# A four-stage network kernel: software-pipelined loop replaced by a written-out order over eight batches

## What is computed

```
x = x + attn_a(layernorm(x))   # 16 heads of 8, rotary q and k, causal over 256 rows
x = x + ffn(layernorm(x))
x = x + attn_b(layernorm(x))   # causal inside groups of 32 rows, q and k rms-normalised
x = x + ffn(layernorm(x))      # same weights as the first ffn
# ffn: h = silu(q4(x) @ q4(w_gate).T) * (q4(x) @ q4(w_up).T); out = q4(h) @ q4(w_down).T
# q4: blocks of 16 scaled by max|x|/6 and rounded to the FP4 grid 0 .5 1 1.5 2 3 4 6
```

## Time and profile before

| | us |
|---|---|
| median of 3 runs | 627.68 |
| lowest and highest run | 624.8, 632.15 |
| span of the profiled execution | 621.5 |
| VectorE busy / TensorE busy / ScalarE busy | 354.9 / 387.6 / 203.7 |
| mean granted TensorE clock | 0.834 |

### The profile page before, as it was taken

The page is one execution under the profiler, slowest core; times in us unless marked ns, Lnnn a source line. Parts: engine busy times, 40 slices in busy tenths (PEclk is TensorE's granted clock), DMA queues, the critical chain, the costliest instruction groups (busy, mean ns, idle before and its releaser), DMA issues.

```text
span 621.5 us, 11084 instructions
## 1 busy us (share of the span) xinstructions
PE 387.6 (62%) x4031; PEld 249.4 (40%) x4061; DVE 354.9 (57%) x950; ACT 203.7 (33%) x548; POOL 168.9 (27%) x210
## 2 busy tenths in 40 slices
PE   0316656756966796678677866785788438516533
PEld 0214434534543554455444544454445324303312
DVE  3406667267249844985497449755954637431532
ACT  1000603512640374146404640564155204302300
POOL 6110210430243044214430443143222212320201
PEclk9957969968895999599968996998689759955955
DMA  5050140072018002800370037004600130040000
GB/s 170 0 120 2 32 90 2 23 159 47 1 52 170 6 2 65 165 3 0 88 141 3 0 84 146 3 0 102 122 4 2 45 66 3 9 102 2 10 0 8
DMA packets 61951, 31.84 MB, mean 51 GB/s; under 512 B 3360, under 2 KB 61664, under 8 KB 61920
## 3 DMA queue, kind: packets, MB, share of 16 engines
q1 hardware_dynamic: 61920, 31.42, 22.9%
HBM read 17.19 MB, written 13.63 MB: 50 GB/s over the span
## 4 chain that ended last, share of the span: by engine, by line
PE 44%; DVE 25%; issue 8%; DMA 6%; POOL 6%; ACT 6%; SPq 4%; POOLq 0%; DVEq 0%; ACTq 0%
PE bank L619 6%; PE bank L637 4%; PE bank L517 3%; PE bank L585 3%; PE bank L577 3%; PE bank L502 3%; PE bank L465 3%; DMA Kl<-scr_l 2%; DVE bmax L972 2%; PE bank L432 2%; PE bank L444 2%; PE bank L506 2%; PE bank L630 2%; PE bank L572 2%; PE bank L541 2%
## 5 line engine op out<-in xcount | busy, mean ns | idle before, releaser
L972 DVE TENSOR_REDUCE bmax<-bank 128x3 f32<-128x384 f32 x128 | 63.0, 552 | 24.1 <-PE bank L487 22.8
L693 ACT ACTIVATE prob<-bank 128x384 f32<-128x384 f32 x128 | 55.9, 490 | 12.1 <-PE bank L506 11.0
L483 PE MATMUL bank<-Kf,Qf 128*128 128x128 bf16 x128 | 23.5, 281 | 53.9 <-DMA Kf<-scr_f 45.7
L828 POOL TENSOR_TENSOR fa__w<-fa__w,fa__c 128x256 f32<-128x256 f32 (+1 forms) x16 | 19.2, 1202 | 116.4 <-DVE fa__w L932 116.4
L828 POOL TENSOR_TENSOR fb__w<-fb__w,fb__c 128x256 f32<-128x256 f32 (+1 forms) x16 | 19.9, 1242 | 92.9 <-DVE fb__w L932 92.9
L733 ACT ACTIVATE probl<-bank 128x512 f32<-128x512 f32 x64 | 38.3, 599 | 19.2 <-PE bank L577 18.1
L483 PEld LDWEIGHTS bank<-Kf,Qf 128*128 128x128 bf16 x128 | 10.1, 113 | 72.5 <-DMA Kf<-scr_f 30.9
L485 PE MATMUL bank<-Kf,Qf 128*128 128x256 bf16 x128 | 35.5, 374 | 0.0
L487 PE MATMUL bank<-maskb,identb 128*128 128x256 bf16 x128 | 34.9, 369 | 0.0
L577 PE MATMUL bank<-Ql,Kl 51*128 51x128 bf16 x256 | 26.1, 224 | 11.7 <-DMA Ql<-nmTl 9.5
L656 ACT ACTIVATE fa__xqT<-bank 128x256 f32<-128x256 f32 x8 | 3.1, 385 | 84.1 <-PE bank L432 84.1
(11 more groups left out here) (208 smaller groups left out, 966.4 us busy)
## 6 DMA issues: line engine op xcount, KB each, us to landing
scr_f<-partsf SPq DMA_DIRECT2D x16, 192.0 KB, 2.3
Qf<-scr_f SPq DMA_DIRECT2D x16, 192.0 KB
Kf<-scr_f SPq DMA_DIRECT2D x16, 192.0 KB
scr_l<-partsl SPq DMA_DIRECT2D x16, 192.0 KB, 3.4
Ql<-scr_l SPq DMA_DIRECT2D x16, 192.0 KB, 3.6
Kl<-scr_l SPq DMA_DIRECT2D x16, 192.0 KB, 4.9
scr_f<-partsf SPq DMA_DIRECT2D x16, 128.0 KB, 2.0
scr_l<-partsl SPq DMA_DIRECT2D x16, 128.0 KB, 2.2
```

Of the source, the lines that this page charges most:

```text
L693: act.activation(prob[:, h % 8, :], bank[h % 3][:, 0:384], ACT.Exp).then_inc(f.s_exp, 1)
L828: pool.tensor_tensor(w.w[:, 0:n], w.w[:, 0:n], w.c[:, 0:n], ALU.subtract).then_inc(dif, 1)
L972: dve.tensor_reduce(bmax[:, h, :], bank[h % 4][:, 0:384].rearrange("p (n k) -> p n k", k=P), AX.X, ALU.max).then_inc(bmax_done, 1)
```

## The change

The kernel after has no loop and no passes: every stage of every batch is a generator of its own, and `weave` puts the segments of an engine in the order of a table of ranks (`TIMES`), one line a batch. The table takes, on each engine, among the segments that can run, the one of the oldest batch. The FFN banks (now 6 and 7; the local stages have 4 and 5) are handed on in the order `FFN_TURNS`: up and down of one FFN, then the next FFN. The residual stays in one tile `xall` for all batches, loaded once, all at the start, and each block adds into it; the copies L1039, L995 and L908 and the second load of x are gone. `Qf`, `Kf`, `Ql`, `Kl` and `Vl` have two homes each, which GpSimd fills at the start. The x-side of the FFN quantisation has tiles of its own (`xu`, `xc`, `xw`, `xscale`). The local scores of batch b now wait for the end of x3 of batch b-1, and the shifted local scores of batch b for the split (`s_rest`) of batch b+1, since local1 of the next batch uses the same two banks between them. All weight quantisation stands near the start, before the scores of batch 0. The matmuls, the exponentials and the FFN arithmetic are the same, instruction for instruction.

```diff
-F1K = dict(load=-47.98, ln=-112.26, turn=-33.14, qkv=-5.62, rope=9.99, split=65.11, fetch=31.52)
...
-LAG = 4
+FFN_TURNS = [
+    ("a", 0, "up"), ("a", 0, "down"), ("a", 1, "up"), ("a", 1, "down"),
...
+    ("b", 2, "up"), ("b", 2, "down"), ("a", 6, "up"), ("a", 6, "down"),
...
+TIMES = {
...
+    "pe.front2": """
+3 4 5 6 7 8 9 10 13 14 15 16 17 18 19 20 21 22 23 24 25 26
...
-def merge(*threads):
...
+def weave(engine, threads):
+    steps = []
+    for n, (stage, b, thread) in enumerate(threads):
+        next(thread)
+        at = TIMES[engine + "." + stage].splitlines()[1 + b].split()
+        steps += [(float(t), n, k) for k, t in enumerate(at)]
+    for _, n, _ in sorted(steps):
+        next(threads[n][2], None)
...
-        xin = sb("xin", [P, T, D])
-        xres = sb("xres", [P, T, D])
+        xall = sb("xall", [P, NBATCH, T, D])
...
-        Qf = sb("Qf", [P, H, SEQ], BF16)
-        Kf = sb("Kf", [P, PAIRS, SEQ], BF16)
+        Qfs = [sb(f"Qf{i}", [P, H, SEQ], BF16) for i in range(2)]
+        Kfs = [sb(f"Kf{i}", [P, PAIRS, SEQ], BF16) for i in range(2)]
...
+        Vls = [sb(f"Vl{i}", [P, T, H, VW]) for i in range(2)]
...
+        def turn_before(w, b, phase):
+            n = FFN_TURNS.index(("a" if w is ffn_a else "b", b, phase))
...
+            return (w0.s_h_ready if phase0 == "up" else w0.s_done), T * (b0 + 1)
...
+        def passes(engine, **stages):
+            threads = []
+            for stage, thread in stages.items():
+                threads += [(stage, b, thread(b)) for b in range(1 if stage == "weights" else NBATCH)]
+            weave(engine, threads)
...
-                if later(b):
-                    sp.wait_ge(f.s_st_ps, b * H)
+                if b > 1:
+                    sp.wait_ge(f.s_st_ps, (b - 1) * H)
...
-                if later(b):
-                    pe.wait_ge(l.s_done, b)
-                turn(bank[7], flat(xnl)).then_inc(l.s_xnT_ps, 1)
+                if b > 0:
+                    pe.wait_ge(l.s_nmT, b)
+                    if b > 1:
+                        pe.wait_ge(l.s_done, b - 1)
+                turn(bank[5], flat(xnl)).then_inc(l.s_xnT_ps, 1)
...
+                pe.wait_ge(l.s_rest, b + 1)
+                if b > 0:
+                    pe.wait_ge(l.s_done, b)
...
+                            if b < NBATCH - 1:
+                                pe.wait_ge(l.s_rest, b + 2)
...
-                elif both:
-                    pe.wait_ge(ffn_a.s_h_ready, T * (b + 3))
-                turn(bank[5], w.xq).then_inc(w.s_xqT_ps, 1)
+                if (turn_of := turn_before(w, b, "up")) is not None:
+                    pe.wait_ge(*turn_of)
+                turn(bank[6], w.xq).then_inc(w.s_xqT_ps, 1)
...
-                dve.tensor_copy(rs[:, 0, :], stats[:, :, 0])
...
-                link(dve.tensor_copy(xl[:, :, :], x2[:, :, :]))
-                moments(link, l, xl, stl, mvl, rsl)
+                moments(link, l, res(b), stl, mvl)
...
-                dve.wait_ge(xres_loaded, (b + 1) * 16)
-                dve.tensor_tensor(flat(x1), bank[2][:, 0:T * D], flat(xres), ALU.add).then_inc(f.s_done, 1)
+                dve.tensor_tensor(flat(res(b)), bank[2][:, 0:T * D], flat(res(b)), ALU.add).then_inc(f.s_done, 1)
```

More of the change, by code:

```diff
@@ L49 @@
[L49 to L54 removed]
+FFN_TURNS = [
[8 rows of a table added]
+]
@@ new lines @@
+TIMES = {
+    "sp.front1": """
+0 1
+3 4
+6 7
+12 13
+18 19
+24 26
+31 32
+38 39""",
+    "sp.front2": """
+2
+5
+11
+17
+23
+30
+37
+44""",
+    "sp.local1": """
+8 9
+14 15
+20 21
+25 28
+33 35
+40 42
+45 47
+49 50""",
+    "sp.local2": """
+10
+16
+22
+29
+36
+43
+48
+52""",
+    "sp.store": """
+27
+34
+41
+46
+51
+53
+54
+55""",
+    "pe.weights": """
+2""",
+    "pe.front1": """
+0 1
+11 12
+38 39
+74 75
+123 127
+171 175
+225 226
+280 281""",
+    "pe.front2": """
[7 rows of a table added]
+314 315 317 321 323 326 328 330 336 341 343 344 346 348 350 351 352 354 356 360 363 365""",
+    "pe.local1": """
@@ new lines @@
+397 400 404 407 409
+412 415 419 426 427
+428 429 430 431 432""",
+    "pool.front1": """
+0 2 3 4
+5 6 7 8
+9 13 15 17
+18 25 26 28
+29 38 39 41
+42 50 53 56
+57 64 65 68
+69 78 79 82""",
+    "pool.front2": """
+1
+10
+19
+32
+45
+59
+72
+85""",
+    "pool.local1": """
+16 20 22
+27 30 31
+40 43 44
+52 54 58
+67 70 73
+81 83 86
+92 93 95
+101 102 104""",
+    "pool.ffn_a1": """
+11 12
+21 23
+33 34
+46 47
+60 61
+74 75
+87 88
+96 97""",
+    "pool.ffn_a2": """
+14
+24
+37
+49
+63
+77
+90
+99""",
+    "pool.ffn_b1": """
@@ new lines @@
+35 36
+48 51
+62 66
+76 80
+89 91
+98 100
+106 107
+109 110""",
+    "pool.ffn_b2": """
+55
+71
+84
+94
+103
+105
+108
+111""",
+    "dve.weights": """
+0 2 3 4 5 6 7 8 10 11 13 15 16""",
+    "dve.front1": """
+1 9 12
+14 17 35
+36 37 65
+67 72 104
+105 110 149
+151 154 193
+195 206 243
+244 250 294""",
+    "dve.front2": """
[7 rows of a table added]
+311 312 314 316 318 319 320 321 322 323 325 326 328 330 340 341 342 355 357""",
+    "dve.local1": """
+70 71 74 77
+108 109 111 112
+152 153 155 156
+196 198 203 204
+247 249 255 256
@@ new lines @@
+297 299 304 305
+345 347 352 353
+376 378 382 384""",
+    "dve.local2": """
+93 123 127
+131 167 171
+175 221 227
+231 278 282
+285 324 329
+333 362 364
+367 390 392
+395 406 407""",
+    "dve.ffn_a1": """
+40 43 45 47
+76 79 81 83
+115 118 120 122
+159 162 164 166
+210 213 215 217
+261 264 266 268
+310 313 315 317
+358 359 360 361""",
+    "dve.ffn_a2": """
+56 60 62 64 66 68 69
+91 94 96 98 100 106 107
+130 133 135 137 139 148 150
+174 177 179 181 183 192 194
+225 230 233 235 237 245 246
+277 281 283 287 289 295 296
@@ L399, in ffn2 @@
-            def ffn2(w, b, s):
-                yield w.keys["d1"]
-                if w is ffn_b:
-                    sp.wait_ge(w.s_done, w.ahead + T * (b + 1))
-                    sp.dma_start(batch(out, b), x4[:, :, :]).then_inc(out_stored, 16)
-            passes(sp, front1, front2, local1, local2, nothing, ffn2)
-            sp.wait_ge(out_stored, NBATCH * 16 + 16)
+                yield
+                if b > 1:
+                    sp.wait_ge(l.s_st_ps, (b - 1) * 2 * GROUPS)
+                fetch(b, l, scr_l, Qls[b % 2], Kls[b % 2])
@@ new lines, in local1, with store @@
+                yield
+            def local2(b):
+                yield
+                max_rows(b, l, nmTl, Qls[b % 2])
+                yield
+            def store(b):
+                yield
+                sp.wait_ge(ffn_b.s_done, T * (b + 1))
+                sp.dma_start(batch(out, b), res(b)).then_inc(out_stored, 16)
+                yield
+            passes("sp", front1=front1, front2=front2, local1=local1, local2=local2, store=store)
+            sp.wait_ge(out_stored, NBATCH * 16)
@@ L598, in local2, with ffn2 @@
                 mm.then_inc(l.s_proj_ps, 1)
-            def ffn2(w, b, s):
-                first = w is ffn_a
-                both = not isinstance(s, int) or LAG <= s < NBATCH + 2
-                yield w.keys["turn"]
+                yield
+            def ffn2(w, b):
+                yield
                 pe.wait_ge(w.s_xq_ready, b + 1)
-                if first:
-                    done_b = max(s - LAG, 0) if isinstance(s, int) else s - LAG
-                    pe.wait_ge(ffn_b.s_done, T * done_b + ffn_b.ahead)
+                if w is ffn_a and b == 0:
@@ L1071 @@
+                yield
+            passes("dve", weights=weights, front1=front1, front2=front2, local1=local1, local2=local2,
+                   ffn_a1=lambda b: ffn1(ffn_a, b), ffn_a2=lambda b: ffn2(ffn_a, b),
+                   ffn_b1=lambda b: ffn1(ffn_b, b), ffn_b2=lambda b: ffn2(ffn_b, b))
 _INS = ['L0_attn_a_x', 'L0_attn_a_Wq', 'L0_attn_a_Wk', 'L0_attn_a_Wv', 'L0_attn_a_Wo', 'L0_attn_b_w_qkv',
```

675 lines of the change are left out of this document (366 added, 309 removed), and 40 rows, old and new, of tables (FFN_TURNS, TIMES).

## The result

The changed kernel takes 645.14 us (median of 4 runs, 644.77 to 645.52), the kernel before in the same session 626.24 us: a ratio of 1.0301, 95% interval 1.0233 to 1.0368. The forecast was 547 us with a range of 506 to 590, so both the sign and the range were wrong.

A forecast was written before the change was run, and what follows sets the result against it. Neither TensorE nor VectorE fills the pass; the order between them bounds it. From 621.5 us: steady state -54, filling -22, start +3, drain -7 give 541 us of span, with 6.2 us more 547; range 506 to 590.

The forecast's parts named there:

- the period: Steady state: 41.8 us of TensorE work a batch at 83% busy gives 50 us a batch, before 60.8.
- Only the waits go: Rival for the steady state: the pass loses only the stack's wait and the copies, 55 us a batch, 572 us; chance 0.15.
- FFN banks bind: Rival: one FFN holds banks 6 and 7 until done, 29 us each, 58 us a batch, 586 us; chance 0.15.
- a fixed order that fits badly: Sign of a wrong forecast: x1 sums 55 us or more apart, TensorE's waits for VectorE spread over every chain.
- Slower: Rival: serial FFN banks, in-order engines hold back each FFN's next step; at 36 us an FFN 657 us; chance 0.04.
- Two homes: Steady state: with two homes for the stack the next batch's fetch skips the wait for shifted scores; TensorE waited 3.94 us.
- the filling: Batches 1 and 2, x1 of batch 0 to batch 2: stack waits -14, overlap -8, so 83 us instead of 105.1.
- The start: Up to x1 of batch 0: more weight quantisation before the first centring, +3 us, bounds 0 and +6; GpSimd's fills hidden.
- The drain: From x1 of batch 7 to the end: a chain of latencies, 126 us instead of 133.1, bounds 118 and 133.
- The clock: TensorE's granted clock, 0.68 in the thin part before, stays near 1.00 until x1 of batch 7.
- the idle time of the earlier trace: At the loop's pass boundary: TensorE's 4.33 us idle weight load lies beside the wait for `Kf` and adds nothing.
- the copies: VectorE's copies that go: 1.7 us a batch, so its work falls from 41.1 to 39.4 us.

The follow-up runs named there:

- replan_oldest: The changed kernel with only its order table remade on all five engines, oldest batch first, from measured durations; 589.2 us, ratio 0.9411.
- plan_serial: The changed kernel with second-home fills later and all five engines' order searched from measured durations, FFN turns kept; 566.5 us, ratio 0.9002.
- change_one_home: The changed kernel, order untouched, with one home each for Qf, Kf, Ql and Kl and fewer fills at the start; 640.6 us, ratio 1.0230.
- fills_later: The changed kernel with GpSimd's fills of the second homes moved behind its part of front1 of batch 0; 639.0 us, ratio 1.0227.
- one_home: The changed kernel with interleaved FFN turns, one home for each stack and an order searched for that; 541.1 us, ratio 0.8538.

## Why the prediction was wrong

**The step that failed: the period.** "TensorE reached 83% where three chains were interleaved; I take this for the whole: 41.8 / 0.83 = 50 us a batch." The work was right: 42.9 us of TensorE in the 61.0 us shown above against 41.8 predicted, and 40.65 of VectorE against 39.4. What was wrong is the share, 70% in place of 83%. It was read as a property of the mixture of work. It is a property of the order: the same code ran at a period of 61.2 us in the change and of 51.2 us in replan_oldest, with TensorE 80% busy, and plan_serial, with the same turns, reached the 83% and a period of 51.2 us, close to the 50 predicted. The 83% came from a stretch whose order fitted, and I took over the number without its order. The table was in the diff and the durations in the trace, so for each engine one could have laid out which instruction waits behind which; whether that would have given 61 us was not tried.

**The rivals.** *Only the waits go* had the mechanism, "the fixed order doesn't overlap maxima and dense work", but priced the result as the old period less the waits removed, 55 us. It did not allow that a wait taken away comes back under another name: -35 us for `Kf`, +44 us for `bmax`. *FFN banks bind* gave 58 us a batch, near the 61.2 measured, but its sign is missing: the x turn of the second FFN waits only 0.5 us for the sum of the first, and the banks stand free for 10.6 us in the period shown. The sign that came true is the last one in the prediction, a fixed order that fits badly, though the waits for `bmax` come once in a period and not in every chain. *Slower* was held at 0.04 and had the time nearly right (657), by a mechanism that holds only in part: FFNs in series took 24 to 28 us each in the drain, not 36, and the turns cost about 17 us, less than the table. That its time was near is mostly luck.

**Two homes.** "With two homes for the stack, the fetch of the next batch no longer waits": in the kernel before it never did wait for the shifted scores. The home was free 10 us before the fetch began, and second homes are worth nothing in the change (change_one_home 640.6, fills_later 639.0). The late split held the fetch up, and in the new order it comes earlier. In the filling 7.0 us were counted twice for the stack, but batch 2 waited only 3.7 us of them, and what the stack's wait gave back other waits took: x1 of batch 0 to x1 of batch 2 took 103.3 us, 83 predicted, 105.1 before.

**The start.** +3 us predicted, +12 measured. The weight steps ahead of the first centring cost 1.7 us, inside the bounds of 0 and +6. Left out was that GpSimd's first steps are slower beside the weight steps that follow, which with 1.7 us makes the scores 4.0 us late, and x1 of batch 0 5.6. The fills, "hidden behind VectorE until 25.8", cost 6.3: they end at 19 us, near the 20 computed, but VectorE stood still beside them.

**The drain.** 126 us predicted, 143.4 measured. x1 to x2 of batch 7 (33.9 us, 34 predicted), the last FFN (32.9, 31.5) and the store (3.2, 2.3) came out; x2 to x3 took 73.4 us, 58 predicted. The new waits themselves are short, 1.5 us in all for `restl` and 1.3 for x3. The work between them is what grew: x2 to the split 17.2 us (12.5 predicted), the shifted scores of batch 6 up to x3 24.6 (18.5), and from there to x3 of batch 7 31.4 (27). What was left out is that four FFNs of stage b, of batches 4 to 7, come after x1 of batch 7 where before it was three; they hold the banks for 24 to 28 us each, and their steps stand among those of the local attention in TensorE's row. TensorE has 84.65 us of work in this drain, 59.8 before. How the 15 us divide among these steps was not tested. Its two largest waits there:

```profile
PE bank L896 <- POOL fa__u L1104: 10.6, 1, 10.6
PE bank L896 <- POOL fb__u L1104: 10.5, 3, 9.4
```

Both are for the quantised h of the one FFN that holds the banks.

**The clock.** "Near 1.00 until x1 of batch 7": it was 0.89 in the period shown and 0.87 over the five batches, 0.94 in replan_oldest and in plan_serial, and 1.00 in the best period of one_home. The direction of the reasoning held where the order did.

**Right:** the loop is free, the idle time of the earlier trace rows is not to be counted twice, the copies are small, and TensorE's work per batch (42.9 us in the period shown, 43.8 in the mean of the five).

## What to carry to other kernels

When a change replaces an order on in-order engines, price the order, not the edits. Lay each engine's rows out against measured durations before believing any overlap (no run here shows how near that would have come). Make the table from the profile of the code that it is for and run more than one, for a greedy plan is fragile (one code and one rule ran at 589, 624 and 646 us). Don't move the visibly late steps of one engine alone; the engines' rows lock into each other, and the wait returns elsewhere. Before buying a second buffer, look in the queue that fills it: if what stands ahead of the fetch is something else than the old contents being in use, a second buffer can't help.
